# A recurrence and a quantised feed-forward on one core: the states' scale from the uncorrected maximum, and products of the first group between the late corrections

## The chip, the core and the metric

One core of a Trainium2 chip runs the whole kernel. The metric is the device time of one execution in microseconds; for the kernel before it is the median of three runs. The engines are TensorE (PE; its weight loads are PEld), VectorE (DVE), ScalarE (ACT), GpSimd (POOL) and SyncE (SP, whose queue issues most of the transfers).

## The reference, cut to what matters

The data are `x` of 2 x 2048 x 512 floats. A recurrence runs over the 2048 time steps of both sequences, and its states go through a feed-forward layer of two products (512 to 2048 and back), with weights in int8 steps and activations in uint8 steps:

```python
xW = jnp.einsum('ntd,dh->nth', x, Wx) + b
next_h = jnp.tanh(xw_t + prev_h @ Wh)              # 2048 steps
def quant_act_uint8(x):
    s = jnp.maximum(jnp.max(x), EPS) / 255.0       # one scale for the whole tensor
    return jnp.clip(jnp.round(x / s), 0.0, 255.0) * s
h = relu(quant_linear(states, w1, b1))             # quantises the states, then the product
y = x + quant_linear(h, w2, b2)                    # quantises h
factors = {'cond_1024': 8.0, ...}                  # the start state is a normal times 8
```

What matters here: the scale of the states needs the largest of all states, and the first product of the feed-forward needs the scale.

## The kernel before, in words

**Recurrence.** The time axis is cut into 64 chunks per sequence, so 128 columns (64 chunks x 2 sequences) go through 32 steps together (`STEPS`). A state of a step is 128 partitions x 4 x 128 columns. Columns 0 and 1 (`BATCH`) start from the true start state; the other 126 (`SEAM`) start from a guess, made beside the first stage (x times Wx) by running the last 20 steps in f16. `main_pass` then runs all 32 steps in f32 (L621, L627). Now the last state of each chunk is known well, and the state with which the next chunk was started was only the guess. So 12 corrections follow (`FIXED`): for step t, `lay_fixed(t)` on ScalarE puts the sums of step t into the bank (L1052), `fix_step(t)` on TensorE adds the f16 weights times the error of the step before (16 products of 126 columns, L647), `fix_tanh(t)` on ScalarE takes tanh in two halves (L1059), and `fix_pair(t, a)` on VectorE makes the new error from each half (L1347). VectorE also takes the maximum of each corrected step (L1357).

**The seam check and the scale.** After correction 12, `largest_state` reduces all maxima to one column (L1384); `spread_stat` on TensorE turns it (L753) and spreads the largest over 128 partitions (L756), with VectorE's reduction of the row between (L1393). `judge_seams` and `count_seams` (L1388, L762) decide whether the corrections were enough; VectorE writes a flag (L1405), and each of TensorE, ScalarE and VectorE loads it (`load_flag`) and branches past a `repair`, which isn't taken with these inputs. Meanwhile `keep_going` lets TensorE do 5, 2 and 1 products that nobody reads (L574). `quantise_first` (L1445) makes the first group's integers in four instructions, one for each k.

**Feed-forward.** Tokens are in 8 groups of 512 (four steps each). `TURNS` is the order of the groups, `tokens(g)` says which steps group g holds. A group's first product is 16 tiles of 128x512 (`f`), each 4 products (`k`), in pairs of tiles (L794); ScalarE keeps them with bias and scale (`keep_pair`, L1098) and VectorE takes a maximum of each pair (L1526). Two pairs (`UNCHECKED = 2`, 16 products) may run before the flag is known. VectorE quantises two groups ahead (`AHEAD`, L1512). Three of the groups (`SPILLED`) are written out to DRAM by SP and fetched again in the second half. There are four slots for kept groups (`STORED_AT`), which lie over states that are no longer needed. The second product (L859) starts when the hidden scale is known.

In the kernel before the first group is group 5, the first four corrected steps:

```python
TURNS = (5, 6, 7, 3, 0, 1, 2, LAST)
def tokens(g): return (g + FIRST_GROUP) % GROUPS     # FIRST_GROUP is 3
UNCHECKED = 2
IDLE_STATES = (5, 2, 1)
```

Of the kernel before, what the change touches and what calls it, by code (L numbers as in the profile page):

```python
# [5 lines left out]
ALU = mybir.AluOpType  # L6
# [8 lines left out]
AX_XY = mybir.AxisListType.XY  # L15

# [74 lines left out]
TURNS = (5, 6, 7, 3, 0, 1, 2, LAST)  # L91


def tokens(g):

    return (g + FIRST_GROUP) % GROUPS

STORED_AT = {5: 0, 6: 3, 7: 0, 3: 3, 0: 0, 1: 1, 2: 2}

Q_SLOT = (0, 1, 2, 3, 6, 5, 4, 7)  # L100
# [8 lines left out]
UNCHECKED = 2  # L109
# [28 lines left out]
IDLE_STATES = (5, 2, 1)  # L138
# [5 lines left out]
STAT_LINKS = 6  # L144


def rnn_ffn_program(nc, xT, h0T, wx, wh, bT, w1, b1T, w2, b2T, ident, yT):
    with ExitStack() as ctx:
# [46 lines left out]
        seam_diff = part(after_fixed + 3584, 512).rearrange("p (k c) -> p k c", k=KT)  # L195

# [13 lines left out]
        q_first_ints = part(rings, KT * GTOK // 2, U16).rearrange("p (k t) -> p k t", k=KT)  # L210
        q_first = part(rings, KT * GTOK // 2, F16).rearrange("p (k t) -> p k t", k=KT)
# [50 lines left out]
        seam_over = sb("seam_over", [P, 3], F32)  # L262
        ones_col = sb("ones_col", [P, 1], F32)
        redo_flag = sb("redo_flag", [1, 1], I32)
# [60 lines left out]
        state_ready = sem("state_ready")  # L325
        fixed_laid = sem("fixed_laid")
# [12 lines left out]
        seams_counted = sem("seams_counted")  # L339
        q_again = sem("q_again")  # L340
        made_again = sem("made_again")
        flag_ready = sem("flag_ready")
# [3 lines left out]
        sc_link = sem("sc_link")  # L346
        q_ready = sem("q_ready")
# [35 lines left out]
        def load_flag(engine):  # L383
            return engine.value_load(redo_flag[:, :], min_val=0, max_val=P)

        def while_seams_differ(engine, flag, repair, then=lambda: None):

            with engine.If(flag != 0):
                with engine.Fori(1, CHUNKS) as r:
                    again = load_flag(engine)  # L390
                    with engine.If(again != 0):
                        repair(r)
                then()
# [27 lines left out]
        def _(sp):  # L421
# [51 lines left out]
            for s, g in enumerate(SPILLED):  # L473
                for n in range(QUARTERS):

                    sp.wait_ge(acc_kept, ACC_RING + s * PAIRS + (n + 1) * per)
# [88 lines left out]
        def _(pe):  # L565
# [76 lines left out]
            def fix_step(t):  # L642

                at, par = 4 * (t % 2), (t - 1) % 2

                def add(j, k):
                    return nc.tensor.matmul(bank[:, at + j, BATCH:COLS],  # L647
                                            wh_high[:, k, j * P:(j + 1) * P],
                                            error[:, par, k, 0:SEAM], start=False,
# [100 lines left out]
            def spread_stat(n, meanwhile=lambda: None):  # L750

                pe.wait_ge(stat_ready, n + 1)
                nc.tensor.transpose(bank[0:1, 0, 0:P], stat[:, :], id32[:, :]).then_inc(stat_turned, 1)  # L753
                meanwhile()
                pe.wait_ge(row_ready, n + 1)
                nc.tensor.matmul(bank[:, 1, 0:1], ones[:, :], stat_row[:, :], start=True,  # L756
                                 stop=True).then_inc(stat_spread, 1)

            def count_seams(n, width):

                pe.wait_ge(seams_judged, n + 1)
                nc.tensor.matmul(bank[0:1, 2, 0:width], ones_col[:, :], seam_over[:, 0:width],  # L762
# [10 lines left out]
            for t in range(1, FIXED + 1):  # L773
                fix_step(t)
# [11 lines left out]
            def first_pair(states_in, pair, made, by_k=False, last=False):  # L786

                tiles = [(f, k) for f in (2 * pair, 2 * pair + 1) for k in range(KT)]
                if by_k:
                    tiles.sort(key=lambda t: t[1])  # L790
                for f, k in tiles:
                    if by_k and f == 0:
# [863 lines left out]
```

## Time and profile before

| what | value |
|---|---|
| median of 3 runs | 495.73 us (495.28 to 497.13) |
| profiled execution: its time | 497.24 us |
| its span | 495.2 us |
| mean granted TensorE clock | 0.995 |
| main pass, 32 steps | 123.6 to 239.3 us |
| corrections on TensorE | 240.77 to 260.97 us |
| first product of the feed-forward | 264.77 us |
| second product | 381.01 us to the end |

The profile is that of one execution. The span is the time from its first to its last instruction; the execution's own time is 2.0 us longer. Times in rows are in us from the start of the span.

### The profile page before, as it was taken

How to read it: one execution, taken by the hardware profiler on the slowest of the kernel's cores; microseconds unless marked ns; L12 is line 12 of the kernel's file. 1: busy time of each engine (PE TensorE's matmuls, PEld its weight loads, DVE VectorE, ACT ScalarE, POOL GpSimd, SP SyncE). 2: the span in 40 equal slices, each digit the busy share in tenths (PEclk: the TensorE clock that was granted, in tenths of full speed). 3: DMA queues.
4: the chain of work that ended last, by engine and by line, in shares of the span. 5: the costliest groups of instructions: out<-in, count | busy, mean ns of one | idle time of the engine just before them, and what ended most of it. 6: DMA issues, size and time to landing. Idle time of an engine off the chain costs nothing.

```text
span 495.2 us, 8656 instructions
## 1 busy us (share of the span) xinstructions
PE 477.0 (96%) x3003; PEld 326.1 (66%) x3003; DVE 295.5 (60%) x476; ACT 236.2 (48%) x450; POOL 94.1 (19%) x69
## 2 busy tenths in 40 slices
PE   8998999999999999999659999999999999999997
PEld 3687888888999999999654444444443444444443
DVE  2789846457333355454779877888768433454443
ACT  0325454454323333332673888888884334343340
POOL 2843190400000000000000000000000554534355
PEclk9999999999999999999998999999999999999999
DMA  8974422200457000000000777200002189888883
GB/s 292 387 261 169 171 87 86 85 1 1 95 100 143 0 1 0 0 0 0 2 1 3 323 292 318 86 0 1 0 1 85 45 294 314 298 285 292 314 316 129
DMA packets 38165, 65.37 MB, mean 132 GB/s; under 512 B 19056, under 2 KB 19200, under 8 KB 34560
## 3 DMA queue, kind: packets, MB, share of 16 engines
q1 hardware_dynamic: 37472, 64.04, 37.4%
q10 hardware_dynamic: 576, 1.05, 0.6%
q8 instruction: 12, 0.20, 0.2%
q14 instruction: 9, 0.07, 0.0%
q0 software_dynamic: 96, 0.01, 0.0%
HBM read 39.93 MB, written 20.97 MB: 123 GB/s over the span
## 4 chain that ended last, share of the span: by engine, by line
PE 90%; DVE 6%; ACT 1%; issue 1%; DMA 1%; DVEq 0%; ACTq 0%
PE bank L794 22%; PE bank L859 22%; PE bank L584 14%; PE bank L621 12%; PE bank L627 12%; PE bank L611 3%; PE bank L669 3%; PE bank L647 2%; DVE arena L1203 1%; DVE arena L1347 1%; DVE w_absmax L1196 1%; ACT arena L1059 1%; DMA arena<-x_t 1%; DVE arena L1252 0%; DVE arena L1567 0%
## 5 line engine op out<-in xcount | busy, mean ns | idle before, releaser
L560 POOL TENSOR_SCALAR arena<-arena,bq 128x512 f32<-128x512 f32 x32 | 53.3, 1680 | 337.7 <-DVEq L1610 286.0
L794 PE MATMUL bank<-arena,w_words 128*128 128x512 f16 (+1 forms) x512 | 112.4, 383 | 0.7 <-DVE arena L1445 0.7
L859 PE MATMUL bank<-arena,w2t 128*128 128x512 f16 x512 | 110.7, 379 | 0.5 <-DVE arena L1573 0.5
L1098 ACT ACTIVATE arena<-bank,bq,s_bits 128x512 f32<-128x512 f32 x124 | 89.6, 774 | 28.6 <-PE bank L794 22.9
L794 PEld LDWEIGHTS bank<-arena,w_words 128*128 128x128 f16 x512 | 50.5, 99 | 62.2 <-issue 1.6
L859 PEld LDWEIGHTS bank<-arena,w2t 128*128 128x128 f16 x512 | 49.7, 98 | 61.5 <-DVE arena L1567 2.0
L1526 DVE TENSOR_REDUCE hid_parts<-arena 128x1 f32<-128x1024 f32 x60 | 72.5, 1218 | 21.8 <-ACT arena L1098 21.2
L621 PE MATMUL bank<-arena 128*128 x512 | 63.5, 277 | 0.0
L627 PE MATMUL bank<-arena 128*128 x512 | 62.4, 275 | 0.0
L621 PEld LDWEIGHTS bank<-arena 128*128 128x128 f32 x512 | 59.7, 192 | 0.6 <-issue 0.4
L627 PEld LDWEIGHTS bank<-arena 128*128 128x128 f32 x512 | 59.7, 192 | 0.0
L1157 ACT ACTIVATE arena<-arena,s_hid_inv 128x1024 uint16 (+1 forms) x31 | 35.4, 1145 | 47.8 <-PE bank L859 47.2
L584 PE MATMUL bank<-arena,w_words 128*128 128x256 f32 x224 | 53.4, 383 | 1.2 <-DVE arena L1252 1.2
L1573 DVE TENSOR_SCALAR arena<-arena,s_hid_inv 128x1024 uint16 (+1 forms) x31 | 25.1, 813 | 40.3 <-PE bank L859 40.1
L584 PEld LDWEIGHTS bank<-arena,w_words 128*128 128x128 f32 x224 | 41.5, 190 | 6.8 <-DVE arena L1252 1.6
L1311 DVE TENSOR_TENSOR bank<-bank,arena 128x128 f32<-128x128 f32 x80 | 24.0, 300 | 36.4 <-PE bank L627 27.6
L1032 ACT ACTIVATE arena<-bank 128x128 f32 (+1 forms) x80 | 22.2, 278 | 48.5 <-DVE bank L1311 45.9
L584 PE MATMUL bank<-arena 128*128 128x256 f32 x168 | 40.2, 381 | 0.0
L927 ACT ACTIVATE arena<-bank,b_sb 128x256 f32<-128x256 f32 x56 | 23.4, 468 | 29.9 <-PE bank L584 29.9
L584 PEld LDWEIGHTS bank<-arena 128*128 128x128 f32 x168 | 31.3, 190 | 4.4 <-issue 0.4
L1304 DVE TENSOR_TENSOR arena<-bank,arena 128x128 f32 x48 | 14.0, 292 | 29.9 <-PE bank L627 29.4
L1252 DVE TENSOR_TENSOR arena<-bank,arena 128x512 f32<-128x512 f32 x21 | 14.3, 690 | 27.3 <-PE bank L584 26.8
(104 smaller groups left out, 355.8 us busy)
## 6 DMA issues: line engine op xcount, KB each, us to landing
spill<-arena SPq DMA_DIRECT2D x12, 1024.0 KB, 3.9
arena<-spill SPq DMA_DIRECT2D x12, 1024.0 KB, 8.3
arena<-w SPq DMA_DIRECT2D x8, 1024.0 KB, 5.1
arena<-x_t SPq DMA_DIRECT2D x32, 256.0 KB, 4.0
y_t<-arena SPq DMA_DIRECT2D x32, 256.0 KB, 2.1
arena<-x_t SPq DMA_DIRECT2D x7, 1024.0 KB, 8.6
arena<-x_t ACTq DMA_DIRECT2D x4, 256.0 KB, 5.8
arena<-wx SPq DMA_DIRECT2D x4, 256.0 KB, 5.4
```

Source lines behind the costliest of these rows:

```text
L560: nc.gpsimd.tensor_scalar(xb[:, d], xb[:, d], bq2[:, d:d + 1], None, ALU.add).then_inc(xb_ready, 1)
L584: mm = nc.tensor.matmul(bank[:, at, j * HALF:(j + 1) * HALF], weights[:, k, j * P:(j + 1) * P], x_half[:, k, :], start=(first and j == 0 a ...
L621: nc.tensor.matmul(bank[:, at + j, 0:COLS], wh_sb[:, k, j * P:(j + 1) * P], state(k), start=(k == 0), stop=False)
L627: mm = nc.tensor.matmul(bank[:, at + j, 0:COLS], wh_sb[:, k, j * P:(j + 1) * P], state(k), start=False, stop=(k == KT - 1))
L794: mm = nc.tensor.matmul(bank[:, f % 8, :], w1t[:, k, f * P:(f + 1) * P], states_in[:, k, :], start=(k == 0), stop=(k == KT - 1))
L859: return nc.tensor.matmul(bank[:, 4 + d, :], w2t[:, f, d * P:(d + 1) * P], hq[:, f % HQ_RING, :], start=(f == 0), stop=(f == FT - 1))
L927: nc.scalar.activation(out[:, :, j, :], bank[:, chain_bank(i), j * HALF:(j + 1) * HALF].rearrange("p (s c) -> p s c", c=COLS), ACT.Identit ...
L1098: kept = nc.scalar.activation(out[:, e, :], bank[:, (f + e) % 8, :], ACT.Identity, bias=bq1[:, f + e:f + e + 1], scale=s1_bits[:, f + e:f ...
L1157: made = nc.scalar.activation(hidden[:, f % HQ_RING:f % HQ_RING + 2, :], src, ACT.Relu, scale=s_hid_inv[:, 0:1])
L1311: nc.vector.tensor_tensor(z, z, xw[:, s, j, :], ALU.add).then_inc(sum_ready, 1)
L1526: nc.vector.tensor_reduce(hid_parts[:, columns:columns + 1], source, AX_XY, ALU.max).then_inc(kept_seen, 1)
L1573: nc.vector.tensor_scalar(hidden[:, f % HQ_RING:f % HQ_RING + 2, :], source, s_hid_inv[:, :], 0.0, ALU.mult, ALU.max).then_inc(own_ready, 1)
```

## The change

The kernel after takes the scale of the states from a maximum that is known before the corrections: `largest_unfixed` reduces the maxima of all 32 uncorrected steps, the last two together in one instruction; TensorE turns it after correction 1 (`turn_stat(0)`) and spreads it after correction 2 (`spread_guess`). The first group is now group 1, whose steps (12 to 15) aren't corrected. VectorE makes its integers beside corrections 2 to 4 and the scales and biases of the first sums beside 4 to 6. TensorE issues 22 of the group's 64 products behind corrections 5 to 12, and 34 more behind the last one, before it waits for the flag (`UNCHECKED = 14` tiles). ScalarE keeps the first two tiles behind corrections 9 to 11 and ten in all before the flag. The corrections use banks 4 to 7 only, two at a time, so that the first group can use 0 to 3; `lay_fixed(1)` comes after the last tanh of the main pass. The maxima of corrected steps 2 to 6 are taken beside corrections 7 to 11, those of 7 to 12 after the last. After the true maximum is known, it is compared with the guessed one (`ALU.not_equal`) and counted with the seams; where they differ, scale, integers and the 56 products are made again. The idle products `IDLE_STATES` are gone, and the reduction of the first error moves behind the corrections. VectorE now also takes the maximum of each of the first 12 steps in the main pass.

```diff
-TURNS = (5, 6, 7, 3, 0, 1, 2, LAST)
+TURNS = (1, 5, 6, 7, 3, 0, 2, LAST)
+TOKENS = (5, 3, 6, 4, 7, 0, 1, 2)
 def tokens(g):
-    return (g + FIRST_GROUP) % GROUPS
+    return TOKENS[g]
-UNCHECKED = 2
+UNCHECKED = 14
+UNCHECKED_KEPT = 10
+FIRST_BANK = (0, 1, 2, 3, 0, 1, 6, 4, 5, 2, 3, 0, 1, 6, 4, 5)
+SCALE_ROW_BANK, SCALE_BANK = 0, 1
+ROW_BANK, COUNT_BANK = 7, 7
+BESIDE_FIX = {5: (0, 3), 6: (3, 6), 7: (6, 9), 8: (9, 12), 9: (12, 15), 10: (15, 16),
+              11: (16, 19), 12: (19, 22)}
+def first_tile(i):
+    return (i + 2) % FT
-IDLE_STATES = (5, 2, 1)
...
-            for t in range(1, FIXED + 1):
-                fix_step(t)
             pe.wait_ge(w2_turned, 16 * KT)
...
+            for at in range(4, 8):
+                bits = nc.tensor.matmul(bank[:, at, 0:2 * COLS], w1t[:, 0, 0:P],
+                                        w1t[:, 0, 0:2 * COLS], start=True, stop=True)
+            bits.then_inc(fix_bits_set, 1)
...
+            fix_step(1)
+            turn_stat(0, SCALE_ROW_BANK)
+            fix_step(2)
+            spread_guess()
+            for t in range(3, FIXED + 1):
+                fix_step(t)
+                if t in BESIDE_FIX:
+                    unchecked_products(*BESIDE_FIX[t])
+
+
+            unchecked_products(BESIDE_FIX[FIXED][1], 6 * KT)
             pe.wait_ge(fixed_ready, 2 * (FIXED - 1))
-            keep_going(IDLE_STATES[0])
-            spread_stat(0, lambda: keep_going(IDLE_STATES[1]))
-            keep_going(IDLE_STATES[2])
-            count_seams(0, 3)
...
+            unchecked_products(6 * KT, 7 * KT)
+            pe.wait_ge(fixed_ready, 2 * FIXED)
+            unchecked_products(7 * KT, 9 * KT)
+            turn_stat(1, ROW_BANK)
+            unchecked_products(9 * KT, 12 * KT)
+            count_seams(0, 4)
+            unchecked_products(12 * KT, UNCHECKED * KT)
...
             late_step(0, STEPS - 2, 0)
+            late_step(0, STEPS - 1, 1)
+            act.wait_ge(fix_bits_set, 1)
             lay_fixed(1)
-            late_step(0, STEPS - 1, 1)
             lay_fixed(2)
...
             for t in range(1, FIXED + 1):
                 fix_tanh(t)
                 if t + 2 <= FIXED:
                     lay_fixed(t + 2)
+
+                if t == FIXED - 3:
+                    act.wait_ge(sums_scale_ready, 1)
+                    act.wait_ge(acc_ready, 1)
+                    keep_first(0, slice(0, HALF))
+                elif t == FIXED - 2:
+                    keep_first(0, slice(HALF, GTOK)).then_inc(first_kept, 1)
+                elif t == FIXED - 1:
+                    keep_first(1).then_inc(acc_kept, 1)
+            first_pairs_kept(1, UNCHECKED_KEPT // 2)
...
+            def largest_unfixed():
+
+                linked(nc.vector.tensor_reduce(slot_max[:, STEPS - 1:STEPS],
+                                               states[:, STEPS - 1:STEPS + 1, :, :], AX_XYZ,
+                                               ALU.max), error_link, 1)
+                nc.vector.tensor_reduce(stat[:, :], slot_max[:, 1:STEPS], AX_X,
+                                        ALU.max).then_inc(stat_ready, 1)
...
+            def beside_step(t):
+                if t == 1:
+                    largest_guess()
+                    largest_fixed(1)
+                elif t == 2:
+                    dve.wait_ge(stat_spread, 1)
+                    state_scale(stat_link, 0)
+                    quantise_first(0, q_ready)
+                elif t == 3:
+                    quantise_first(1, q_ready)
+                    quantise_first(2, q_ready)
+                elif t == 4:
+                    quantise_first(3, q_ready)
+                    scale_of_sums(chain)
+                elif t == 5:
+                    bits_of_sums(chain)
+                    bias_steps(chain, b1_sb, s1_inv, t1)
+                elif t == 6:
+                    quantised_bias(chain, bq1, b1_sb, s1, t1)
+                    dve.sem_inc(sums_scale_ready, 1)
+                else:
+                    largest_fixed(t - 5)
...
+            add_late(STEPS - 1, 0, STEPS - 1)
+            first_errors()
+            largest_unfixed()
+            for t in range(1, FIXED):
+                for a in range(2):
+                    fix_pair(t, a)
+                beside_step(t)
+            fix_pair(FIXED, 0)
             fix_pair(FIXED, 1)
-            largest_row(0)
-            last_seam()
-            dve.wait_ge(error_link, 4)
+            for t in range(FIXED - 5, FIXED):
+                largest_fixed(t)
+            for a, slot in ((0, FIXED), (1, STEPS)):
+                last = nc.vector.tensor_reduce(slot_max[:, slot:slot + 1],
+                                               fixed[:, FIXED - 1, 2 * a:2 * a + 2, :], AX_XY, ALU.max)
+            linked(last, error_link, 2)
+            largest_state(STEPS + 1)
...
+            nc.vector.tensor_tensor(seam_over[0:1, 3:4], stat_row[:, :], guess_row[:, :],
+                                    ALU.not_equal)
             judge_seams(3)
-            state_scale(0)
             raise_flag(0, 3)
-
-            quantise_first(q_ready)
```

`unchecked_products(first, end)` issues the products `first` to `end - 1` of the group, four to a tile, each tile in its own bank of `FIRST_BANK`, after the tile that held the bank was kept.

## Rows read from the trace of the kernel before

**Rows 1.** The page: busy time of the engines, and the chain by engine.

```profile
PE 477.0 (96%) x3003; PEld 326.1 (66%) x3003; DVE 295.5 (60%) x476; ACT 236.2 (48%) x450; POOL 94.1 (19%) x69
...
PE 90%; DVE 6%; ACT 1%; issue 1%; DMA 1%; DVEq 0%; ACTq 0%
```

**Rows 2.** Windows: stretch, length, busy of each engine (instructions), granted clock, DMA share, GB/s.

```profile
245.00:250.00 5.00, 2.92 (x49) 2.50 (x46) 3.86 (x10) 3.95 (x9) 0.00 (x0) 1.00 0.00 0
260.97:264.77 3.80, 2.61 (x14) 0.97 (x12) 3.45 (x13) 0.42 (x2) 0.00 (x0) 1.00 0.00 0
264.77:266.50 1.73, 1.73 (x5) 0.67 (x6) 1.66 (x6) 0.00 (x0) 0.00 (x0) 0.59 0.04 9
266.50:268.30 1.80, 1.80 (x5) 0.61 (x4) 1.44 (x8) 0.09 (x1) 0.00 (x0) 0.50 0.03 9
...
280.00:375.40 95.40, 95.40 (x444) 43.24 (x442) 75.12 (x76) 76.86 (x107) 0.00 (x0) 1.00 0.26 107
```

**Rows 3.** The timeline at the start of the corrections: start, duration, idle before.

```profile
239.62 0.68 DVE L1316 TENSOR_REDUCE slot_max<-arena  x1
...
240.06 0.60 ACT L1052 ACTIVATE bank<-arena 128x512 f32<-128x512 f32 x1
...
240.77 1.04 PE L647 MATMUL bank<-arena 128*128 128x126 f16 x16 [1.51 <-ACT bank L1052]
...
241.94 0.75 DVE L1347 TENSOR_TENSOR arena<-arena 128x252 f16<-128x252 f32 x2
...
242.60 0.68 DVE L1357 TENSOR_REDUCE slot_max<-arena 128x1 f32<-128x512 f32 x1
243.20 0.68 DVE L1359 TENSOR_REDUCE slot_max<-arena 128x1 f32<-128x512 f32 x1
```

**Rows 4.** The timeline of one correction in steady state.

```profile
247.25 0.75 DVE L1347 TENSOR_TENSOR arena<-arena 128x252 f16<-128x252 f32 x2 [0.38 <-ACT arena L1059]
247.58 0.60 ACT L1052 ACTIVATE bank<-arena 128x512 f32<-128x512 f32 x1
...
247.81 1.04 PE L647 MATMUL bank<-arena 128*128 128x126 f16 x16 [0.69 <-DVE arena L1347]
...
248.56 0.72 ACT L1059 ACTIVATE arena<-bank 128x256 f32<-128x256 f32 x2 [0.38 <-PE bank L647]
```

**Rows 5.** The timeline from the last tanh to the first products.

```profile
260.68 0.71 ACT L1059 ACTIVATE arena<-bank 128x256 f32<-128x256 f32 x2 [1.02 <-PE bank L647]
...
260.81 1.24 PE L574 MATMUL bank<-w_words 128*128 128x512 f16 x5
...
261.43 0.74 DVE L1368 TENSOR_REDUCE slot_max<-arena 128x1 f32<-128x256 f32 x2
262.21 0.19 DVE L1384 TENSOR_REDUCE stat<-slot_max 128x1 f32<-128x33 f32 x1
...
262.45 0.27 PE L753 MATMUL bank<-id,stat 128*1 128x128 f32 x1 [0.40 <-DVE stat L1384]
...
264.17 0.15 DVE L1405 TENSOR_REDUCE redo_flag<-bank 1x1 int32<-1x3 f32 x1
264.25 1.65 DVE L1445 TENSOR_SCALAR arena<-arena,s_in_inv 128x512 uint16<-128x512 f32 x4
...
264.77 20.42 PE L794 MATMUL bank<-arena,w_words 128*128 128x512 f16 x86 [0.71 <-DVE arena L1445]
...
265.88 0.23 DVE L1498 TENSOR_SCALAR s<-w_scale,s_in 128x16 f32<-128x16 f32 x1
...
268.02 3.26 DVE L1512 TENSOR_SCALAR arena<-arena,s_in_inv 128x512 uint16<-128x512 f32 x8 [0.15 <-DVE bq L1494]
```

**Rows 6.** Groups by line and shape, whole span: count, busy us, mean ns, idle before.

```profile
L1526 DVE TENSOR_REDUCE hid_parts<-arena 128x1 f32<-128x1024 f32 x60 | 72.5, 1218 | 21.8 <-ACT arena L1098 21.2
...
L927 ACT ACTIVATE arena<-bank,b_sb 128x256 f32<-128x256 f32 x56 | 23.4, 468 | 29.9 <-PE bank L584 29.9
```

**Rows 7.** The timeline: two tiles kept by ScalarE.

```profile
270.12 1.45 ACT L1098 ACTIVATE arena<-bank,bq,s_bits 128x512 f32<-128x512 f32 x2 [0.47 <-PE bank L794]
```

More of the change, by code:

```diff
@@ L15 @@
 AX_XY = mybir.AxisListType.XY
+AX_XYZ = mybir.AxisListType.XYZ
 P = 128
@@ L778, in keep_going @@
                 idle_products(n, at, w1t[:, 0, 0:P], w1t[:, 0, 0:GTOK])
-            pe.wait_ge(fixed_ready, 2 * (FIXED - 1))
-            keep_going(IDLE_STATES[0])
-            spread_stat(0, lambda: keep_going(IDLE_STATES[1]))
-            keep_going(IDLE_STATES[2])
-            count_seams(0, 3)
[L786 to L792, printed above, removed]
-                        pe.wait_ge(q_ready, k + 1)
-                    mm = nc.tensor.matmul(bank[:, f % 8, :], w1t[:, k, f * P:(f + 1) * P],
-                                          states_in[:, k, :], start=(k == 0), stop=(k == KT - 1))
-                    if last and f == FT - 2 and k == KT - 1:
+            for at in range(4, 8):
+                bits = nc.tensor.matmul(bank[:, at, 0:2 * COLS], w1t[:, 0, 0:P],
+                                        w1t[:, 0, 0:2 * COLS], start=True, stop=True)
@@ new lines, in _, with first_product, unchecked_product @@
+            bits.then_inc(fix_bits_set, 1)
+            def first_product(f, k, states_in, at):
+                return nc.tensor.matmul(bank[:, at, :], w1t[:, k, f * P:(f + 1) * P],
+                                        states_in[:, k, :], start=(k == 0), stop=(k == KT - 1))
+            def unchecked_product(n, made):
+                i, k = n // KT, n % KT
+                mm = first_product(first_tile(i), k, q_first, FIRST_BANK[i])
+                if i % 2 == 1 and k == KT - 1:
+                    mm.then_inc(made, 1)
@@ new lines, in wait_tile_kept, with unchecked_products @@
+            def wait_tile_kept(i):
+                if i % 2 == 0:
+                    pe.wait_ge(first_kept, i // 2 + 1)
+                else:
+                    pe.wait_ge(acc_kept, ACC_RING + i // 2 + 1)
+            def unchecked_products(first, end):
+                for n in range(first, end):
+                    if n < KT:
+                        pe.wait_ge(q_ready, n + 1)
+                    if n % KT == 0 and holder_of(n // KT) is not None:
+                        wait_tile_kept(holder_of(n // KT))
+                    unchecked_product(n, acc_ready)
@@ L797, in first_pair @@
+            turn_stat(1, ROW_BANK)
+            unchecked_products(9 * KT, 12 * KT)
+            count_seams(0, 4)
+            unchecked_products(12 * KT, UNCHECKED * KT)
+            def first_pair(states_in, pair, last=False):
+                for f in (2 * pair, 2 * pair + 1):
+                    for k in range(KT):
+                        mm = first_product(f, k, states_in, f % 8)
+                    if last and f == FT - 2:
                         mm.then_inc(half_ready, 1)
-                mm.then_inc(made, 1)
@@ L800, in first_products @@
[L800 to L802 removed]
+                mm.then_inc(acc_ready, 1)
+            def first_products(turn, states_in, last=False):
+                for pair in range(PAIRS):
                     pe.wait_ge(acc_kept, turn * PAIRS + pair + 1)
[L805 to L809 removed]
+                    first_pair(states_in, pair, last=last)
@@ L1322, in early_steps, with late_steps @@
                         add_early(first + s + par, 4 - 4 * par, s + par)
-                        if largest:
-                            largest_of(first + s + par, s + par)
-            def late_steps(first):
-                with dve.Fori(FIXED // 2, STEPS // 2) as half:
+                        largest_of(first + s + par, s + par)
+            def late_steps(first, until):
+                with dve.Fori(FIXED // 2, until // 2) as half:
                     s = half * 2
```

326 lines of the change are left out of this document (190 added, 136 removed).

## The prediction, made before the change ran

> **What bounds the kernel now.** I read the page first, then the chain that ended last, then the windows around the seam between the recurrence and the first feed-forward product, then the timeline there. The page shows TensorE busy for 477.0 of 495.2 us and 90% of the chain on it [rows 1]. So only two things can shorten this kernel: filling time in which TensorE waits or runs slowly, or taking work off it. The change takes no product away (64 products of the first group stay 64), so I look for waiting and slow time. There are three places, all between 240.8 and 268.3 us.
>
> First, the twelve corrections. In steady state one takes 1.73 us, and TensorE waits 0.69 us in each for VectorE's next error; over 5 us it was busy 2.92 [rows 2, 4]. Second, the tail: the last correction's stream is over at 260.81, where the idle products start, and the first real product starts at 264.77 [rows 5]. In the 3.96 us between, TensorE only turns and spreads a maximum and runs eight products whose result nobody reads. Third, from 264.77 to 268.3 the granted clock is 0.59 and 0.50, the 1.2 GHz level, after that tail; before it and in the long stretch after it is 1.00 [rows 2]. In that long stretch a 128x512 product costs 95.40 / 444 = 0.215 us. The 86 products from 264.77 took 20.42 us; 86 x 0.215 is 18.5 and about 0.2 is the drain of the last, so the low clock cost 1.7 us [rows 2, 5]. Product 64 therefore ended at 264.77 + 13.76 + 1.7 = 280.2.
>
> After it the stage is TensorE's: 100% busy from 280 to 375.4, VectorE 75.12 and ScalarE 76.86 of 95.40 [rows 2]. What the first group gains is kept to the end, if neither of these falls far behind.
>
> **The start of the corrections.** Before, the clearing of the first correction's bank ran ahead of the last tanh; now both clearings follow it. ScalarE does one at 240.06 to 240.66 already, the place that the first now takes [rows 3]. TensorE's first correction started at 240.77; with 0.14 us from the end of a releasing instruction to TensorE (from VectorE's pair that starts at 247.25, each 0.42, to TensorE at 247.81, [rows 4]) it starts at 240.80: +0.03. Four 128x256 products that set the bits of the banks, half of 0.215 each, cost 0.43 before that, while ScalarE does the last tanh: hidden. Without that cover they would cost those 0.43.
>
> VectorE drops the 0.68 us maximum at 239.62, so the two first errors start about 0.55 earlier (the second needs the last tanh, over before 240.06) and end at 240.5. Then comes the new maximum over 1024 columns, 1.22 [rows 6], and one like the 0.19 at 262.21 [rows 5]: done at 241.9, when the first corrected pair is due (241.94 in [rows 3]). No delay. The transpose and the one-column product go onto TensorE into the waits after corrections 1 and 2, 0.27 us for the first as at 262.45 [rows 5], the second shorter in columns but with fp32 weights, together under the 0.69 of each wait. The second maximum beside correction 1 goes away: with it VectorE was taken until 243.20 + 0.60 = 243.80, 0.13 past the beat (241.94 + 1.73 = 243.67); a 128-column one on one partition comes, shorter: -0.1 [rows 3].
>
> The maxima that VectorE now takes in the first twelve steps of the main pass are like the last one of the other twenty, at 239.62, 0.68 us in time in which it waits for TensorE: 0, or 0.68 a step without that wait.
>
> **VectorE beside the corrections.** Between a pair and the next it has a 0.68 maximum and 0.38 idle, 1.06 us [rows 3, 4]. The new contents: scale, as two chained small operations at most 0.5, and one quantisation 0.41 (1.65 / 4, [rows 5]), 0.9; two quantisations 0.82; one and two chained 16-column operations, 0.41 + 0.5 = 0.91; four chained, nine took 2.14 from 265.88 to 268.02, so 0.24 each, 0.95; three, 0.7; then maxima as before. All fit in 1.06. Price 0, with 0.1 a step for three steps if the waits between chained operations are worse.
>
> **TensorE beside the corrections.** Three products are 0.645 us in a wait of 0.69; nineteen stand before correction 12, three behind it. Bounds: 0 hidden, 19 x 0.215 = 4.1 if every one pushed its correction back. I take 0, since the wait of the weight loads is longer than the matmuls' modelled wait, and VectorE and ScalarE, not TensorE, set the step.
>
> **ScalarE beside the corrections.** In a step it has two tanh, 0.71, one clearing, 0.60, and 0.38 idle [rows 4]. After corrections 9 and 10 half a tile (256 columns) is kept in that idle time. No row shows it; the nearest is a 128x256 with a bias from the first stage, 0.468, the other end half of a whole tile's 0.73 (two take 1.45) [rows 6, 7]. So 0 to 0.09 late, twice; with the start of one more instruction between two tanh I take 0.12 each: +0.25. The whole tile after correction 11 has 1.02 us of idle time [rows 5], and takes 0.73: 0.
>
> Corrections in sum: 0.03 - 0.1 + 0.25, so about +0.2, and TensorE's stream of corrections ends at 261.0.
>
> **The tail goes, and a new wait comes.** Products 20 to 36 follow at once: 261.0 + 17 x 0.215 = 264.65. Their banks are free by then (ScalarE, from 261.6, keeps a tile in 0.73, half of 1.45 in [rows 7], and TensorE needs 0.86 for one). Then stands the transpose of the second maximum, and it is late. VectorE has put off five maxima. From 261.66 + 0.33 it does five at the spacing of 242.60 to 243.20, 0.60, so 3.0, two halves in 0.74, and the 33-column one, 0.19: over at 265.9, and TensorE turns it 0.05 later [rows 3, 5]. TensorE waits 1.3 us with nothing behind the transpose able to pass it, and goes on at 266.1. The other 28 products take 6.02 and the count 0.1: product 64 ends at 272.2, where it was 280.2. That is **8.0 us**.
>
> **The flag.** The count is issued after product 48, 268.7; the flag is up at 269.2 (a matmul and two reductions like that at 264.17, 0.15 each, and two ways between engines, 0.45). Each engine then loads the flag and branches. This was hidden: VectorE wrote the flag at 264.32 and had its next operation after the quantisations at 265.88, so the load costs 0 to 1.56 us [rows 5]; I take 0.8. Queued behind it on ScalarE are the keeps of tiles 10 to 12, 0.73 each, of which the second group's first pair needs banks: 269.2 + 0.8 + 2.2 + 0.15 = 272.35, a wait of 0.15 (0.9 at the bound). On VectorE the second group's quantisation, 1.65, is ready at 271.8: in time, 0.4 late at the bound. TensorE itself has eight products, 1.7 us, over its own load. The Trainium skill (Advanced Engine Details and Errata, Control Flow Timing) gives a compare-and-branch 108 ns; it prices the branch alone, no row here shows it, and if it were nearly all of the load the wait would be 0.
>
> Downstream, VectorE starts the first group's maxima at 273.5, two quantisations after the flag. It works 8 x 1.22 + 1.65 = 11.4 us a group [rows 5, 6] against 13.8, so it is 11 us behind at first and level by the sixth group. ScalarE asks for maxima two groups old, so this price is 0. Spills move with their groups, reuse of a slot is still two groups apart: 0.
>
> **Sum**: 8.0 - 0.15 = 7.85 us. The profiled execution took 497.24 (span 495.2): 489.4 would be its like, span 487.35. The median of the runs before, 495.73, is 1.5 lower; from it I forecast **487.9 us**.
>
> **Rivals.**
> *The clock falls again, or the steps stretch.* The wait of 1.3 us is on TensorE alone and nothing fills it. In 260.97 to 264.77 it was busy 2.61 of 3.80 and the clock fell after it [rows 2]. A second fall costs the same 1.7 and, with 0.75 of load, gives 490.3. Against it: here full-width products stand tight before and behind the wait. The Trainium skill (TensorE: Matmul & The Clock Gate, Part 1) has the clock drop to half after too little activity; by that rule alone it could fall here too. The same 490 comes if a third of the nineteen products show in their steps (1.4) and the load is at its bound. Chance 0.18.
>
> *The wait isn't there.* If VectorE does the put-off maxima in time, 1.3 more is gained: 486.6. Against it: it would need 3 us less than its rows. Or the chain is faster than I count. 0.10.
>
> *The scale is wrong, and it is slower.* The guess is the largest uncorrected value; if the true one differs by a bit, the flag is raised. Then VectorE makes the scale and the four quantisations again (about 2.5 with the passes through TensorE), and TensorE repeats 56 products, 12.0: +14.5, so 502.4. It is all or nothing, one unequal value in the comparison. For it: twelve of thirty-two slots change afterwards in low bits. Against it: the reference multiplies the start state by 8, so that of the first step's sums, in the two columns that aren't corrected, many are far out, where tanh is 1; both maxima hold this 1. 0.05.
>
> *Given back later.* TensorE waits for another engine in the second to fourth group, until nothing is gained: VectorE's lag of 11 us must cost 8. TensorE needs maxima two groups old at the most, so it would have to be 27 us behind: 495.7 less at most 2. 0.03.
>
> **Numbers.** Forecast 0.64, with a range of its own from 487.0 to 489.2 (flag load 0 to 1.56, chained operations, half keeps). The range for 8 in 10 is 486.4 to 490.4: it leaves out the repetition, the giving back, and the tails. A measurement tells about 0.5% (2.5 us) from no change: faster 0.92, same 0.03, slower 0.05.
>
> **What would show it.** Right: corrections still 1.73 apart with three products in each wait and clock 1.00; first product of the group at about 248.9 us, not 264.8; no idle products; a wait of 1.3 us on TensorE before the second transpose, ended by the maximum; no low clock after; VectorE's maxima lagging by a group. Wrong: steps of over 1.9 us with TensorE's wait gone; a low clock near 266 to 269; 56 products issued twice; TensorE waits of over 1 us behind the flag or in groups 2 to 4.

## The result, and the profile after

The changed kernel takes 492.56 us in the median of 8 executions (491.78 to 493.96), the kernel before 496.54 in 8 beside it. The ratio is 0.9927, interval 0.9910 to 0.9943: 3.6 us faster (the medians lie 4.0 apart), where 7.85 were forecast. The direction was right, the size was off by half, and 492.56 lies above the range.

The profiled execution of the changed kernel has a span of 490.5 us (time 492.64). Its timeline beside the corrections, to be read against [rows 4]:

```profile
248.25 0.81 PE L824 MATMUL bank<-arena,w_words 128*128 128x512 f16 x3
248.60 0.75 DVE L1485 TENSOR_TENSOR arena<-arena 128x252 f16<-128x252 f32 x2 [0.22 <-ACT arena L1148]
...
249.17 1.04 PE L684 MATMUL bank<-arena 128*128 128x126 f16 x16
...
250.97 1.04 PE L684 MATMUL bank<-arena 128*128 128x126 f16 x16
...
252.70 1.04 PE L684 MATMUL bank<-arena 128*128 128x126 f16 x16
...
256.46 0.55 ACT L1154 ACTIVATE arena<-bank,bq,s_bits 128x256 f32<-128x256 f32 x1
256.91 0.71 ACT L1148 ACTIVATE arena<-bank 128x256 f32<-128x256 f32 x2
```

Three products (L824) fill the wait of 0.69 us; the matmuls of the corrections no longer show a wait. The step is 1.80 from 249.17 to 250.97 (and was in the one before it), and 1.73 from there to 252.70. ScalarE begins the tanh 0.45 after the half tile at 256.46, and the step stays at 1.73 (256.17 to 257.90). Then the timeline from the last correction on, against [rows 5] (the number in brackets is the idle time before, and what ended it; "issue" means that nothing which the profile shows ended it):

```profile
260.50 3.83 PE L824 MATMUL bank<-arena,w_words 128*128 128x512 f16 x17
...
261.46 3.05 DVE L1491 TENSOR_REDUCE slot_max<-arena 128x1 f32<-128x512 f32 x5
...
265.20 0.19 DVE L1495 TENSOR_REDUCE stat<-slot_max 128x1 f32<-128x32 f32 x1
...
265.44 0.27 PE L790 MATMUL bank<-id,stat 128*1 128x128 f32 x1 [1.10 <-DVE stat L1495]
...
265.55 2.75 PE L824 MATMUL bank<-arena,w_words 128*128 128x512 f16 x12
...
268.36 2.33 PE L824 MATMUL bank<-arena,w_words 128*128 128x512 f16 x10
...
268.54 0.14 DVE L1643 TENSOR_REDUCE redo_flag<-bank 1x1 int32<-1x4 f32 x1
269.95 2.79 ACT L1154 ACTIVATE arena<-bank,bq,s_bits 128x512 f32<-128x512 f32 x4 [1.89 <-issue]
270.02 0.17 PEld L824 LDWEIGHTS bank<-arena,w_words 128*128 128x128 f16 x2 [0.26 <-issue]
270.23 3.26 DVE L1688 TENSOR_SCALAR arena<-arena,s_in_inv 128x512 uint16<-128x512 f32 x8 [1.55 <-issue]
...
273.38 11.83 PE L824 MATMUL bank<-arena,w_words 128*128 128x512 f16 x54 [2.69 <-issue]
```

Up to 270.7 this is the forecast, all of it some half a microsecond early. The 10 products at 268.36 are the 8 behind the count and 2 behind the flag. After product 58, TensorE has nothing for 2.69 us. It waits for no engine there: products 57 to 60 belong to one tile and no wait stands between them. The windows of the changed kernel show the same hole at full clock, and that the stage behind it is again TensorE's (busy time of PE, PEld, DVE, ACT, POOL, then the clock):

```profile
270.69:273.38 2.69, 0.00 (x0) 0.00 (x1) 2.69 (x8) 2.04 (x4) 0.00 (x0) 1.00 0.03 9
273.38:275.00 1.62, 1.62 (x8) 0.80 (x9) 1.62 (x3) 0.11 (x1) 0.00 (x0) 1.00 0.00 0
275.00:369.80 94.80, 94.80 (x441) 42.99 (x440) 79.33 (x81) 76.59 (x106) 0.00 (x0) 1.00 0.33 133
```

What runs there is on the queues. The transfers from 270 to 272 us, by queue (packets, MB, share):

```profile
q8 instruction: 1, 0.02, 3.0%
q14 instruction: 2, 0.02, 2.6%
```

**Two sets of executions.** In the 17 executions of the kernel before that were made beside the last experiments, 12 had a mean granted clock of 0.999 or 1.0 and took 494.96 to 496.37; 5 had 0.995 to 0.997 and took 496.95 to 497.39. The profiled one, 497.24, is of the second kind, and [rows 2] show where the clock was low. The changed kernel has both kinds too: 5 at 1.0, 491.78 to 492.64, and 3 at 0.997, 493.66 to 493.96. Like with like, the change gives 3.3 to 3.5 us: 492.06 in the middle of the five against 495.46 in the middle of the 12 (495.57 in the same set of executions beside experiment 1), and 493.75 against 497.00.

Over all 45 executions of the kernel before that stand beside the experiments, 15 have 0.995 to 0.997, and all of them took 496.94 or more. One at 0.999 took 498.24; no profile shows why. A mean of 0.998 or 0.999 is no sign of slow products: in the profile of experiment 8, at 0.998, the clock falls only behind the last product.

### The profile page after: what moved, and what is told of

The parts are those of the page before. It is cut to its first block, busy times and chain, and to the rows that moved or that the text cites. A ratio compares the mean times of both kernels' runs of the same rounds, so it can differ in the third digit from the quotient of the medians.

```text
span 490.5 us, 8663 instructions
## 1 busy us (share of the span) xinstructions
PE 474.3 (97%) x3000; PEld 324.7 (66%) x3000; DVE 300.7 (61%) x492; ACT 235.6 (48%) x451; POOL 95.5 (19%) x69
## 4 chain that ended last, share of the span: by engine, by line
PE 90%; DVE 6%; issue 2%; ACT 1%; DMA 1%; DVEq 0%; ACTq 0%
PE bank L949 22%; PE bank L824 21%; PE bank L621 14%; PE bank L658 12%; PE bank L664 12%; PE bank L648 3%; PE bank L706 3%; PE bank L684 2%; DVE arena L1332 1%; DVE w_absmax L1325 1%; DMA arena<-x_t 1%; DVE slot_max L1491 1%; DVE arena L1485 1%; ACT arena L1148 1%; DVE arena L1381 0%
## 5 line engine op out<-in xcount | busy, mean ns | idle before, releaser
L597 POOL TENSOR_SCALAR arena<-arena,bq 128x512 f32<-128x512 f32 x32 | 54.7, 1723 | 331.3 <-DVEq L1786 280.4
L824 PE MATMUL bank<-arena,w_words 128*128 128x512 f16 (+1 forms) x512 | 112.3, 379 | 2.7 <-issue 2.7
L1154 ACT ACTIVATE arena<-bank,bq,s_bits 128x512 f32<-128x512 f32 (+1 forms) x125 | 89.7, 771 | 25.1 <-PE bank L824 17.5
L824 PEld LDWEIGHTS bank<-arena,w_words 128*128 128x128 f16 x512 | 49.6, 98 | 61.2 <-issue 3.4
L1702 DVE TENSOR_REDUCE hid_parts<-arena 128x1 f32<-128x1024 f32 x60 | 71.2, 1215 | 15.3 <-ACT arena L1154 14.9
L1743 DVE SCALAR_TENSOR_TENSOR arena<-bank,s_bits,arena 128x512 f32<-128x512 f32 x25 | 17.2, 744 | 22.1 <-PE bank L949 22.1
```

The source lines that it names most:

```text
L597: nc.gpsimd.tensor_scalar(xb[:, d], xb[:, d], bq2[:, d:d + 1], None, ALU.add).then_inc(xb_ready, 1)
L824: return nc.tensor.matmul(bank[:, at, :], w1t[:, k, f * P:(f + 1) * P], states_in[:, k, :], start=(k == 0), stop=(k == KT - 1))
L1154: return nc.scalar.activation(out[:, cols], bank[:, at, cols], ACT.Identity, bias=bq1[:, f:f + 1], scale=s1_bits[:, f:f + 1])
L1702: nc.vector.tensor_reduce(hid_parts[:, columns:columns + 1], source, AX_XY, ALU.max).then_inc(kept_seen, 1)
```

## The experiments

Theory A: behind the flag TensorE branches over the repeated part, and the instructions behind it aren't there yet; the stand is their fetch. Theory B: the stand is the loading of the flag itself. Theory C: it is late work of VectorE or ScalarE. All ratios are to the kernel before. That the 16 KB transfers of q8 carry TensorE's instructions is inferred from where they fall.

**1. No branch bodies.** On all three engines the repair and the repetition, which these inputs never enter, are left out; waits and loads of the flag stay.

```diff
-            while_seams_differ(pe, redo_wanted(pe), repair, first_again)
+            redo_wanted(pe)
```

> The changed kernel with the branch past the repeated part left out on all three engines, and with it the repair and the repeated scale, integers and products (these inputs never enter them); each engine still waits for the flag and loads it. In the changed kernel TensorE issues two products after the flag and then stands for 2.69 us with nothing released to it. Theory A, the instructions behind the branch have to be fetched: the stand is gone, products 57 to 64 follow at once, and the second group is held by the keeps for 0.1 to 0.9 us; the ratio to before goes from 0.9927 to about 0.987 to 0.988 (some 489.5 to 490.5 us). Theory B, the stand is the loading of the flag: it stays at 2 to 2.7 us, ratio 0.9925 to 0.993. Theory C, TensorE waits for VectorE's or ScalarE's late work behind the flag: the stand stays above 1.5 us, since both still load.

Measured: 488.98 us (4 executions, 488.50 to 489.17, all at clock 1.0), ratio 0.9851 (0.9823 to 0.9878). The timeline:

```profile
268.03 9.24 PE L824 MATMUL bank<-arena,w_words 128*128 128x512 f16 x42
...
269.16 5.71 ACT L1154 ACTIVATE arena<-bank,bq,s_bits 128x512 f32<-128x512 f32 x8 [1.42 <-DVE redo_flag L1643]
269.33 3.26 DVE L1688 TENSOR_SCALAR arena<-arena,s_in_inv 128x512 uint16<-128x512 f32 x8 [0.97 <-DVE redo_flag L1643]
```

42 products in a row: no stand and no wait behind the flag. Its queues show no transfer of instructions from 264 to 273 us. B and C are out as the cause of the 2.69, since the loads and the late work are all still there. (The rows lie 0.3 us earlier than those of the changed kernel, because the corrections of this execution started that much earlier, 240.12 against 240.43.) It also shows a second, smaller cost of the branch: ScalarE goes on 0.81 us after the flag's end (268.35) in place of 1.27, VectorE 0.98 in place of 1.55.

**2. A shorter repeated part.** TensorE's 56 repeated products are left out of the body (never entered).

```diff
-                for n in range(UNCHECKED * KT):
-                    ...
-                    unchecked_product(n, made_again)
```

> The changed kernel with the 56 repeated products left out of TensorE's branch body (never entered here); branch, loads, repair and the bodies of the others stay. Theory A in its strict form (what lies behind the branch counts by the length of the body jumped over): the stand of 2.69 us gets shorter by more than 1 us or goes, ratio 0.987 to 0.990. If any taken branch costs one fetch of the code behind it, the stand stays between 2 and 3.2 us, perhaps after another number of products, ratio about 0.993. Theory B: unchanged, 0.993.

Measured: 490.41 us, ratio 0.9872 (0.9842 to 0.9901). The profiled execution started its corrections 0.8 us later than that of the changed kernel, which has nothing to do with the edit; the stand is read from the rows:

```profile
269.19 3.63 PE L824 MATMUL bank<-arena,w_words 128*128 128x512 f16 x16
...
273.05 4.26 PE L824 MATMUL bank<-arena,w_words 128*128 128x512 f16 x19 [0.22 <-ACT arena L1150]
```

All 16 products run through, and 0.22 us is left before the second group, ended by ScalarE's keeps. A branch is still taken, and flag and loads are the same. So it is not the branch as such. A transfer of q8 falls in this profile too, between 271 and 272 us: something is still fetched, but TensorE doesn't get as far as the missing code before it is there.

**3. All 64 products before the flag.**

```diff
-UNCHECKED = 14
+UNCHECKED = 16
```

> The changed kernel with all 16 tiles (64 products) issued before the wait for the flag, not 14. The flag is up at the same time, TensorE has 3.4 us of products behind the count in place of 1.7. Theory A: the fetch starts at the same time and TensorE goes on about 273.4 us, now with product 65: the first group ends 1.3 us earlier than 274.7, ratio about 0.990. Theory B: the same, since a load also starts when the flag is up. Theory C (late work of VectorE and ScalarE): the second group's first product stays where it was, 274.7, ratio 0.993.

Measured: 491.02 us, ratio 0.9896 (0.9867 to 0.9925).

```profile
267.96 3.63 PE L824 MATMUL bank<-arena,w_words 128*128 128x512 f16 x16
...
269.55 4.12 ACT L1154 ACTIVATE arena<-bank,bq,s_bits 128x512 f32<-128x512 f32 x6 [1.89 <-issue]
...
272.67 4.23 PEld L824 LDWEIGHTS bank<-arena,w_words 128*128 128x128 f16 x21 [1.58 <-issue]
...
272.70 4.48 PE L824 MATMUL bank<-arena,w_words 128*128 128x512 f16 x20 [1.11 <-ACT arena L1154]
```

More cover, less stand. The profile puts the 1.11 us down to ScalarE, but only the first part is its own: in experiments 2, 6 and 8 the second group starts 2.26 or 2.27 us after ScalarE's first keep behind the flag, which would be 271.81 here. Product 65 starts 0.89 later, and the weight load before it has idle time that nothing in the profile ended. It comes 4.4 us after the flag's end (268.28), close to the 4.7 of the changed kernel (268.68 to 273.38). TensorE had work for 3.3 us from the flag's end, and that wasn't quite enough. Cover is one of two ways to hide the fetch. A and B predicted the same here.

**4. No products beside the corrections.** All of the first group is issued after correction 12; the scale is still that of the uncorrected states.

```diff
                 fix_step(t)
-                if t in BESIDE_FIX:
-                    unchecked_products(*BESIDE_FIX[t])
...
-            unchecked_products(BESIDE_FIX[FIXED][1], 6 * KT)
+            unchecked_products(0, 6 * KT)
```

> The changed kernel without products behind the corrections: all of the first group's products are issued after the twelfth, and ScalarE keeps its first tiles there too. The scale still comes from the uncorrected maximum. Predicted: corrections keep their 1.73 us; the 19 products (4.1 us) are now paid after them, but the wait of 1.1 us before the second transpose goes, so product 36 ends at 268.3 and everything behind it, the stand after the flag too, moves by 2.9 us or a little less: 495.3 us, ratio 0.998 to 1.0. If the corrections with products beside them were slowed by much (they took 1.80 in two of twelve), a part of it comes back: 0.997.

Measured: 496.67 us (10 executions, 494.48 to 497.67), ratio 1.0000 (0.9979 to 1.0021).

```profile
260.53 7.93 PE L824 MATMUL bank<-arena,w_words 128*128 128x512 f16 x36
...
271.22 2.33 PE L824 MATMUL bank<-arena,w_words 128*128 128x512 f16 x10
...
276.48 8.81 PE L824 MATMUL bank<-arena,w_words 128*128 128x512 f16 x40 [2.92 <-issue]
```

Product 59 starts at 276.48, 3.1 us after the 273.38 of the changed kernel. The scale taken early saves the tail, and the stand takes nearly all of it back; the products in the corrections' waits are what is left as gain. In this run the same two steps take 1.80, without products in them, so TensorE didn't stretch them. In times at like clock the sizes are a little smaller: the four executions at 1.0 have their middle at 494.66, 2.6 us above the changed kernel's 492.06 and 0.9 under the 495.57 of the kernel before. The other six have 0.996 or 0.997 and took 496.58 to 497.67.

**5. The kernel before without branch bodies.**

```diff
-            while_seams_differ(pe, load_flag(pe), repair,
-                               first_again)
+            load_flag(pe)
```

(and the same for the other two engines: repair and repetition, never entered, are left out)

> The kernel before, with the branch bodies (repair and repetition, never entered) left out on all three engines; flag and load stay. In the kernel before TensorE had 16 products issued when the flag came. Theory A: a fetch behind the branch is there too (a 16 KB transfer of the instruction queue began at 267.9 us), but it lay under those products, so taking it away gains nothing: ratio 0.999 to 1.001, within 0.4 us in runs at the same clock. If the branch cost the kernel before as much as the changed one, 2.5 us would go and the ratio would be 0.995.

Measured: 496.60 us (10 executions), ratio 1.0006 (0.9989 to 1.0022). The kernel before fetched in the same place, 266 to 268 us (one transfer of q8 and two of q14), and this one has none from 264 to 275; no time changes. So the fetch is old and cost the kernel before nothing that can be measured; the change uncovered it.

**6. Eight repeated products fewer.**

```diff
-                for n in range(UNCHECKED * KT):
+                for n in range(UNCHECKED * KT - 8):
```

> The changed kernel with 48 products in the repeated part in place of 56 (never entered). Theory A, by position: the code behind the branch moves 16 instructions (8 matmuls with their weight loads) forward, so TensorE runs about 10 products behind the flag, not 2, before it reaches code that isn't there yet, 1.7 us more cover: the stand goes from 2.7 to about 1.0 us, ratio 0.989 to 0.9905. If the length of the jump as such counted, the stand would shrink in proportion, by 8/56 to 2.3 us, ratio 0.992.

Measured: 491.02 us, ratio 0.9884 (0.9859 to 0.9910).

```profile
268.99 3.63 PE L824 MATMUL bank<-arena,w_words 128*128 128x512 f16 x16
...
272.83 0.38 PE L824 MATMUL bank<-arena,w_words 128*128 128x512 f16 x1 [0.22 <-ACT arena L1154]
...
273.96 3.40 PE L824 MATMUL bank<-arena,w_words 128*128 128x512 f16 x15 [0.75 <-issue]
```

Eight products behind the flag finish the first group, one of the second runs, and then TensorE stands 0.75 us in the middle of a tile: after 9 products, where it was 2. The product behind the stand comes 4.65 us after the flag's end (269.31).

**7. Eight repeated products more.**

```diff
                     unchecked_product(n, made_again)
+                for n in range(8):
+                    first_product(2, n % KT, q_first, 2)
```

> The changed kernel with 64 products in the repeated part in place of 56 (never entered). Theory A, by position: the code behind the branch now begins in a stretch that hasn't been fetched, so no product runs behind the flag before the stand, which begins after product 56 and lasts 2.5 to 3.5 us until product 57; a whole stretch is there then, and it doesn't come again soon. Ratio 0.992 to 0.994. By length of the jump: 3.1 us after two products, ratio 0.9935. The two differ in where the stand is: after product 56 or after product 58.

Measured: 494.34 us (5 executions, 492.77 to 494.56), ratio 0.9943 (0.9920 to 0.9966). Three of the five have a clock of 0.996 or 0.997; the two at 0.999 and 1.0 took 492.77 and 493.10.

```profile
268.00 1.90 PE L824 MATMUL bank<-arena,w_words 128*128 128x512 f16 x8
...
273.12 4.47 PE L824 MATMUL bank<-arena,w_words 128*128 128x512 f16 x13 [3.23 <-ACT arena L1156]
```

No product runs behind the flag, and the stand is 3.23 us. The profile puts it down to ScalarE, since a wait for a kept tile stands there; that tile (tile 7) was kept before the flag, so this name is not the cause. Experiments 6 and 7 change only code that never runs, by eight products with their weight loads each way (6 takes two waits out as well). The code behind the branch changes its place by that, and the stand moves with it: after 9, 2 and 0 products. That decides for A, and against the length of the jump. Here the clock fell behind the hole. The changed kernel's three executions at 0.997 would fit that, but none of them was profiled:

```profile
270.00:273.10 3.10, 0.00 (x0) 0.00 (x0) 3.10 (x9) 2.37 (x4) 0.00 (x0) 1.00 0.05 11
273.10:276.00 2.90, 2.88 (x10) 1.16 (x11) 2.90 (x4) 0.50 (x1) 0.00 (x0) 0.73 0.02 6
```

**8. A version that beats both.** The repetition stays, in a short form: the ten tiles that were kept are made again in a loop over pairs, on two banks. All 64 products stand before the flag, the second transpose follows product 42 and the count product 52.

```diff
-UNCHECKED = 14
+UNCHECKED = 16
...
-            unchecked_products(7 * KT, 9 * KT)
+            unchecked_products(7 * KT, 42)
             turn_stat(1, ROW_BANK)
-            unchecked_products(9 * KT, 12 * KT)
+            unchecked_products(42, 52)
             count_seams(0, 4)
-            unchecked_products(12 * KT, UNCHECKED * KT)
+            unchecked_products(52, UNCHECKED * KT)
...
-                for n in range(UNCHECKED * KT):
-                    ...
+                with pe.Fori(0, UNCHECKED_KEPT // 2) as pair:
+                    pe.wait_ge(again_turn, pair + 1)
+                    for e in range(2):
+                        for k in range(KT):
+                            at = k * F + (2 + e) * P
+                            mm = nc.tensor.matmul(bank[:, 4 + e, :],
+                                                  w1_flat[:, bass.ds(pair * (2 * P) + at, P)],
+                                                  q_first[:, k, :], start=(k == 0),
+                                                  stop=(k == KT - 1))
+                    mm.then_inc(made_again, 1)
+                pe.wait_ge(kept_again, UNCHECKED_KEPT // 2)
+                for n in range(UNCHECKED_KEPT * KT, UNCHECKED * KT):
+                    unchecked_product(n, made_again)
```

> A version meant to beat both, with the repetition kept: in the repeated part the ten kept tiles are made in a loop of one pair at a time on two banks (8 products of code instead of 40), all 64 products of the first group stand before the wait for the flag, the second transpose is issued after product 42 in place of 36 (the maximum is ready by then) and the count after product 52. Predicted: no wait of 1.1 us before the transpose, no stand of 2.7 us from the fetch; then the second group is held by its own needs, VectorE's integers and ScalarE's keeps of tiles 10 to 12 behind the flag, until about 271.5 us. Product 65 starts there, 3.2 us earlier than the 274.7 of the changed kernel: 489.0 to 489.5 us, ratio about 0.986. If the loop form or the move brings the fetch back, the stand shows as time in which TensorE waits for nothing, ratio 0.990.

Measured: 489.24 us (5 executions, 489.17 to 490.12), ratio 0.9856 (0.9835 to 0.9877), by that 7.1 us under the kernel before; it is 2.8 us under the 492.06 of the changed kernel at full clock.

```profile
267.53 2.76 PE L826 MATMUL bank<-arena,w_words 128*128 128x512 f16 x12
...
271.39 5.99 PE L826 MATMUL bank<-arena,w_words 128*128 128x512 f16 x27 [1.09 <-ACT arena L1166]
```

Product 65 starts at 271.39, where 271.5 was predicted; 0.4 of that is the earlier start of the corrections in this execution (240.01 against 240.43). What holds it now is ScalarE's keeps behind its own load: ScalarE's first keep starts at 269.13, and 2.26 us from there is what it takes in experiment 6 too (2.27 in experiment 2).

**9. The kernel before with more idle products.**

```diff
-IDLE_STATES = (5, 2, 1)
+IDLE_STATES = (6, 4, 2)
...
             count_seams(0, 3)
+            keep_going(3)
```

> The kernel before, with idle products 6, 4 and 2 in place of 5, 2 and 1 and three more behind the count, in time in which TensorE waited anyway. In executions of the kernel before with a mean granted clock of 0.995 to 0.997 the first products run 3.4 us at half clock; in those with 1.0 they don't. If the low clock is what parts the two sets and comes from too little work in the tail, all executions have 0.998 or more and lie at 495.0 to 496.4 us, none at 497 and above: ratio 0.998. If the clock falls all the same, the two sets stay, ratio 1.0. If the added products push the chain of scales back, up to 0.5 us is added to every execution.

Measured: 496.29 us (12 executions, 495.67 to 496.85), ratio 1.0002 (0.9990 to 1.0014). All 12 have a clock of 0.999 or 1.0, and none lies at 496.9 or above, where 5 of 17 of the kernel before do. Its profile has the full clock from 264 to 270 us, where [rows 2] have 0.59 and 0.50. Counted over all 45 executions of the kernel before, 15 fell, against none of these 12. So the low clock parts the two sets, and work in the tail removes it. In the profile the first product comes 24.49 us after the first correction, where it was 24.00: the added products cost the other executions some 0.5 us, and the median gains nothing.

**10. Only the transpose later.**

```diff
-            unchecked_products(7 * KT, 9 * KT)
+            unchecked_products(7 * KT, 42)
             turn_stat(1, ROW_BANK)
-            unchecked_products(9 * KT, 12 * KT)
+            unchecked_products(42, 12 * KT)
```

> The changed kernel with the second transpose after product 42 in place of 36, and nothing else. Its wait of 1.1 us for the maximum goes: products 36 to 48 run at once, VectorE judges the seams by 267.3 us as before, and the count after product 48, which stood at 268.23, moves to 267.3 to 267.5. The flag, the loads and the fetch follow it, so the stand after product 58 starts and ends 0.8 us earlier: ratio 0.991, about 491.6 us. If the wait was covered by the stand behind it (the end of the stand being set by something else), nothing changes: 0.9927.

Measured: 491.05 us, ratio 0.9900 (0.9878 to 0.9921).

```profile
265.19 0.27 PE L790 MATMUL bank<-id,stat 128*1 128x128 f32 x1
...
267.22 2.33 PE L824 MATMUL bank<-arena,w_words 128*128 128x512 f16 x10
...
272.39 3.84 PE L824 MATMUL bank<-arena,w_words 128*128 128x512 f16 x17 [2.84 <-issue]
```

The flag came earlier, at 267.54 where it was 268.68, and the stand moved with it, from 273.38 to 272.39; 0.3 of this is an earlier start of the corrections (240.16 against 240.43). In times, 491.05 lies 1.0 under the changed kernel's 492.06 at full clock. So the wait of 1.1 us was worth 0.7 to 1.0.

## Why the prediction was off, point by point

**The start and the steps** were forecast at +0.2 us and gave -0.3: TensorE's stream of corrections ended at 260.50, not 260.81. The clearing of the first bank started at 239.78, right behind the last tanh, not at the 240.06 of [rows 3]. The first correction so started at 240.43, 0.34 earlier than before. VectorE's chained operations cost 0.07 in each of two steps, the maximum that went away beside the first correction gave 0.1 as forecast, and the half tiles cost nothing.

**Products in the waits** were rightly taken as hidden. Experiment 4 gives their worth: 3.1 us in the rows (2.6 in times at like clock), the 4.1 of nineteen products less the wait of 1.1 before the transpose.

**The wait before the second transpose** was forecast at 1.3 and was 1.1.

**The flag.** It was up at 268.68 (forecast 269.2). The loads took 1.27 us on ScalarE and 1.55 on VectorE, within the bound of 1.56 but above the 0.8 that I took. For TensorE I wrote that it has "eight products, 1.7 us, over its own load". That held for the load: the two products behind it came at 270.02. **The step that failed** is the price behind the flag: the prediction let nothing come after the load. TensorE stood 2.69 us behind the branch, where the forecast had 0.15, from other causes; a wait of over 1 us behind the flag is one of the signs of being wrong that the prediction names. The bound of 0 to 1.56 was read from VectorE alone, and the 16 products of the kernel before hid TensorE's fetch, so no row of before showed its price. It costs 2.5 us more than forecast, and experiments 1, 2, 6 and 7 show it.

**The base** is the second error. The sum of 8.0 us holds 1.7 us of low clock, which the profiled execution had and the larger part of the executions (30 of 45) hadn't. I took it off the median of 495.73, by its time an execution without it. With that counted out, forecast and measurement come near: 8.0 - 1.7 + 0.5 (earlier corrections and wait) - 2.7 = 4.1, against some 3.5 in executions at clock 1.0; the 0.6 between them I can't place, and starts of executions differ by as much. With the stand gone, experiment 1 measures 489.0, and the 8 executions of the kernel before beside it at clock 1.0 have their middle at 495.6: 6.6 us, where the same sum says 6.8.

**Rivals.** The clock did fall again, in 3 of 8 executions. No profile shows where in them. In the profile of experiment 7 it fell behind the stand; in no profile did a low clock follow the wait before the transpose, which the rival named. The scale was equal and nothing was repeated, and VectorE's lag cost nothing: 94.80 of 94.80 us busy on TensorE.

The Trainium skill (Advanced Engine Details and Errata, ISA Cache) gives instruction lines of 16 KB, 256 instructions each, of which two are held (it notes more memory on TensorE). The transfers of q8 agree in size (12 of them 0.20 MB on the page of the profile of before), and experiments 6 and 7 agree that it is a border in the code that counts; no run here shows how many are held. That section has no time for a jump across such a border; here TensorE stood up to 3.23 us, and the next product came 4.4 to 4.9 us after the flag's end.

## What to carry to other kernels

A branch that is never taken into its body still has a price: what stands behind it may have to be fetched. Keep bodies that are seldom entered short (loops in place of written-out products), and give the engine some 5 us of work that it can do from the flag on: the first product that had to be fetched came 4.4 to 4.9 us after the flag's end, and in experiment 3 the 3.3 us of work were not enough. Where cover is taken away, ask also what it hid on the covered engine itself: the profile of before shows only a transfer on an instruction queue there, and no idle time. And look whether the profiled execution stands for the median, before terms of its clock are taken off the median.

## What the runs showed that I had not expected

- After a branch over a body with 56 written-out products TensorE stood 2.69 us, with 64 it stood 3.23, with 48 it was 0.75, and it didn't stand at all where the body was left out or short. Eight more or fewer matmuls in code that never runs moved the kernel between medians of 491.0, 492.6 and 494.3 us (at full clock 491.0, 492.1 and 492.9).
- The flag's load and branch took 1.27 us on ScalarE and 1.55 on VectorE; without the branch bodies 0.81 and 0.98.
- The clock fell in the kernel before behind a tail in which TensorE was never idle for more than 0.71 us at a stretch, in 15 of 45 executions by their mean clock; with seven more 512-column products in the same tail, in none of 12.
